# Splitting the first 128 tokens' convolution and drives into halves in a spiking decoder kernel, with one ScalarE job moved

## The reference

```
h    = rms(layernorm(x)) * w_norm
conv = conv_b + sum over j of 4: h[t - 3 + j] * conv_w[:, j]
h    = silu(conv)                               # 128 features
q, k, v = h @ wq, h @ wk, h @ wv                # 8 heads; q, k divided by their norms
sd   = h @ w_spike                              # the drives, 512 features
for t in 0 .. 511:                              # a recurrence over time
    mem  = 0.9 * mem + sd[t];  spike = mem > 0.5;  mem = mem - 0.5 * spike
    gates alpha[t], beta[t] from spike and from h;  the state is updated and read
```

## Time and profile before

| what | value |
|---|---|
| median of 3 runs | 1064.17 us (1058.85 to 1065.64) |
| profiled execution | 1070.31 us, span 1067.9 us |
| granted TensorE clock, mean | 0.966 |
| PE busy | 955.9 us, 90% |
| DVE busy | 693.0 us, 65% |
| ACT busy | 499.9 us, 47% |
| POOL busy | 181.4 us, 17% |

### The profile page before, as it was taken

One profiled execution on the slowest core, in us unless ns is written; L12 is line 12 of the kernel. 1 busy time (PEld: TensorE's weight loads), 2 busy tenths in 40 slices (PEclk: granted clock), 3 DMA queues, 4 the chain that ended last, 5 costly groups with the idle time before them and its releaser, 6 DMA issues. The chain is left out here.

```text
span 1067.9 us, 39931 instructions
## 1 busy us (share of the span) xinstructions
PE 955.9 (90%) x16658; PEld 641.8 (60%) x16658; DVE 693.0 (65%) x2418; ACT 499.9 (47%) x1506; POOL 181.4 (17%) x362
## 2 busy tenths in 40 slices
PE   7878769999999999999999887989999999999997
PEld 3333247777777777777777776656446446546542
DVE  2788787889899988988777665245435524724710
ACT  6667412555665555655556455433324324423311
POOL 7100100121121121221212211221210310310300
PEclk8999955999999999999999899989999999999999
DMA  3000000000000000000000104001000000000100
GB/s 99 1 1 1 1 2 3 4 4 4 4 5 4 5 4 4 5 4 4 4 4 5 30 5 129 3 10 28 7 1 23 22 0 18 27 1 4 31 0 10
DMA packets 18650, 13.81 MB, mean 13 GB/s; under 512 B 2491, under 2 KB 17259, under 8 KB 18475
## 3 DMA queue, kind: packets, MB, share of 16 engines
q1 hardware_dynamic: 18475, 11.28, 3.6%
HBM read 7.70 MB, written 1.05 MB: 8 GB/s over the span
## 5 line engine op out<-in xcount | busy, mean ns | idle before, releaser
L1105 PE MATMUL banks<-work 64*64 64x64 f32 x3072 | 100.2, 235 | 18.0 <-DVE gates L784 7.5
L1166 PE MATMUL banks<-work 64*64 64x32 f32 x2560 | 108.3, 224 | 8.9 <-ACT work L1568 5.0
L1166 PEld LDWEIGHTS banks<-work 64*64 64x64 f32 x2560 | 93.2, 139 | 21.7 <-issue 13.7
L203 DVE SCALAR_TENSOR_TENSOR mom<-gates 128x16 f32<-128x16 f32 x512 | 98.6, 193 | 11.2
L199 DVE SCALAR_TENSOR_TENSOR gates<-mom,gates 128x16 f32<-128x16 f32 x512 | 96.3, 188 | 11.9 <-ACT gates L1471 6.2
L784 DVE COPY_PREDICATED gates<-work,banks 128x256 f32<-128x256 uint32 x192 | 102.0, 531 | 1.1
L1498 ACT COPY work<-banks 128x128 f32<-128x128 f32 x160 | 43.6, 272 | 121.0 <-PE banks L1141 120.8
L1105 PEld LDWEIGHTS banks<-work 64*64 64x64 f32 x3072 | 74.8, 139 | 35.7 <-issue 26.0
L789 DVE TENSOR_TENSOR work<-work,banks 128x128 f32<-128x128 f32 x160 | 45.9, 287 | 74.9 <-PE banks L1166 71.5
L1141 PE MATMUL banks<-work,gates 64*64 64x32 f32 x2560 | 72.6, 218 | 6.2 <-issue 5.6
L661 POOL TENSOR_TENSOR mom<-mom 128x4 f32<-128x4 f32 x32 | 6.6, 207 | 418.1 <-ACT work L1547 418.1
(11 more groups left out here) (276 smaller groups left out, 2125.3 us busy)
## 6 DMA issues: line engine op xcount, KB each, us to landing
work<-gates SPq DMA_DIRECT2D x28, 38.5 KB
qT<-in_x_dram SPq DMA_DIRECT2D x4, 256.0 KB, 3.8
work<-in_x_dram SPq DMA_DIRECT2D x4, 256.0 KB, 2.9
out_dram<-work SPq DMA_DIRECT2D x4, 256.0 KB, 2.3
gates<-in_w_ff_dram SPq DMA_DIRECT2D x3, 256.0 KB, 3.6
wv_sb<-in_wv_dram SPq DMA_DIRECT2D x1, 512.0 KB, 4.7
work<-in_w_out_dram SPq DMA_DIRECT2D x1, 512.0 KB, 4.0
gates<-in_x_Wq_dram SPq DMA_DIRECT2D x1, 512.0 KB, 5.0
```

The lines of the kernel that those rows point to most:

```text
L203: ve.scalar_tensor_tensor(neg_mem, mem[:, :, t], 1.0, mem[:, :, t], ALU.is_gt, ALU.subtract)\
L1105: last = pe.matmul(level_out(l)[to, a], KS[rows, n.two, hp], late[rows, hp], start=True, stop=True)
L1166: last = pe.matmul(packed(psXT, l)[rows, a], Z[rows, l - 1, z], second_half(XT[:, n.two], l)[rows, a], start=True, stop=True)
```

## The change

Pair 0 is handled in two halves of 64 tokens (256 columns), and `stairs` moves on ACT from behind `centred(0)` to between `keep_qk(4, 2)` and `keep_h0(3)`. PE runs both half convolutions first, then the four drives of half 0, then those of half 1. The first charge needs only the four copies of half 0; the copies of half 1 are waited for at step 64. All later waits on `h_ok`, `sig_ok`, `conv_mm`, `sd_mm` and `sd_ok` are shifted by the added counts. Half 1 of a drive waits until the copy of half 0 of the same drive is out.

```
 charge(ve, t):
-            if t % PAIR == 0:
-                ve.wait_ge(sd_ok, HP * (t // PAIR + 1))
+            if t == 0:
+                ve.wait_ge(sd_ok, HP)
+            if t == PAIR // 2:
+                ve.wait_ge(sd_ok, drives_of(1))
+            if t and t % PAIR == 0:
+                ve.wait_ge(sd_ok, drives_of(t // PAIR + 1))
...
 vector:
-                keep_h(0)
+                keep_half_h(0)
+                keep_half_h(1)
...
 tensor:
+                def convolve_half(h):
+                    if h == 0:
+                        pe.wait_ge(h0_ok, 1)
+                        pe.wait_ge(consts, 6)
+                        pe.wait_ge(cw_ok, PAD + 1)
+                    for j in range(PAD + 1):
+                        at = h * (PAIR // 2) + j
+                        last = pe.matmul(half_bank(h, 0), conv_diag[:, j, :], h0T[:, :, at:at + PAIR // 2],
+                                         start=j == 0, stop=j == PAD)
+                    last.then_inc(conv_mm, 1)
...
+                def drive_half(n, h):
+                    pe.wait_ge(h_ok, h + 1)
+                    if h:
+                        pe.wait_ge(sd_ok, n + 1)
+                    pe.matmul(half_bank(drive_bank(n), h), wsp_sb[:, n, :], half_pair(hT[:, :], h), start=True, stop=True)\
+                        .then_inc(sd_mm, 1)
...
-                convolve(0)
-                for n in range(HP):
-                    drive_in(n)
+                convolve_half(0)
+                convolve_half(1)
+                for h in range(2):
+                    for n in range(HP):
+                        drive_half(n, h)
                 gate_in(0)
...
 scalar:
+                def soft_half(h):
+                    ac.wait_ge(conv_mm, h + 1)
+                    ac.activation(half_sig(h), half_bank(h, 0), ACT.Sigmoid, bias=v("conv_b")).then_inc(sig_ok, 1)
...
+                def keep_half_drive(n, h):
+                    ac.wait_ge(sd_mm, HP * h + n + 1)
+                    ac.mul(half_pair(aT[:, n], h), half_bank(drive_bank(n), h), 2.0).then_inc(sd_ok, 1)
...
                 centred(0)
-                stairs()
-                soft_conv(0)
-                for n in range(HP):
-                    keep_drive(n)
+                soft_half(0)
+                soft_half(1)
+                for h in range(2):
+                    for n in range(HP):
+                        keep_half_drive(n, h)
                 normal(1)
...
                 soft_conv(2)
                 keep_qk(4, 2)
+                stairs()
                 keep_h0(3)
```

More of the change, by code:

```diff
@@ L150, in zn, with half_sig @@
             return in_pair(kT[:, k], NPAIR - 2)
+        def half_sig(h):
+            return sig(0)[:, :, h * (PAIR // 2):(h + 1) * (PAIR // 2)]
         def sig(k):
@@ L181, in decoder_kernel @@
         NQ_ALL = NQK * NPAIR
-        NSD = HP * NPAIR
         AU_BANK, SS_BANK = 5, 4
@@ L193, in spread_bank, with pairs_of, drives_of, half_pair @@
             return ((0, 1, 6, 7) if k == 0 else (2, 3, 4, 7))[g]
+        def pairs_of(k):
+            return k + 1
+        def drives_of(pairs):
+            return HP * (pairs + 1)
+        def half_pair(t, h):
+            return in_pair(t, 0)[:, :, h * (PAIR // 2):(h + 1) * (PAIR // 2)]
+        def half_bank(i, at):
+            return by_batch(bank[i][:, at * (T // 2):(at + 1) * (T // 2)])
         def charge(ve, t):
             ve.wait_ge(fired, t + 1)
-            if t % PAIR == 0:
-                ve.wait_ge(sd_ok, HP * (t // PAIR + 1))
+            if t == 0:
[4 more added lines that the diff above has]
+                ve.wait_ge(sd_ok, drives_of(t // PAIR + 1))
             ve.scalar_tensor_tensor(mem[:, :, t], neg_mem, -0.9, mem[:, :, t], ALU.mult, ALU.add).then_inc(charged, 1)
@@ L631, in _ @@
                     gp.tensor_copy(EA[:, slot, 0], eye.unsqueeze(1).broadcast_to([P, HP, C])).then_inc(zeroed, 1)
-                gp.wait_ge(h_ok, NPAIR)
+                gp.wait_ge(h_ok, pairs_of(NPAIR))
                 gp.memset(Z, 0.0).then_inc(zeroed, 1)
@@ L689, in row_sums, with keep_half_h @@
                     ve.tensor_scalar(of_pair(neg_mean, k), of_pair(total, k), -1.0 / D, None, ALU.mult).then_inc(mean_ok, 1)
+                def keep_half_h(h):
+                    ve.wait_ge(sig_ok, h + 1)
+                    ve.scalar_tensor_tensor(half_pair(hT[:, :], h), half_bank(h, 0), v("conv_b"), half_sig(h), ALU.add, ALU.mult)\
+                        .then_inc(h_ok, 1)
                 def keep_h(k):
-                    ve.wait_ge(sig_ok, k + 1)
+                    ve.wait_ge(sig_ok, pairs_of(k + 1))
                     ve.scalar_tensor_tensor(in_pair(hT[:, :], k), by_batch(bank[k % 2]), v("conv_b"), sig(k), ALU.add, ALU.mult)\
@@ L1006, in turn_z @@
                     last.then_inc(zn_mm, 1)
+                def convolve_half(h):
[8 more added lines that the diff above has]
+                    last.then_inc(conv_mm, 1)
                 def convolve(k):
                     pe.wait_ge(h0_ok, k + 1)
[L1010 to L1014, removed]
+                    pe.wait_ge(h_ok, (2, pairs_of(k - 1))[k >= 2])
                     for j in range(PAD + 1):
@@ L1018, in convolve @@
                     last.then_inc(conv_mm, 1)
-                def drive_in(n):
[L1021 to L1026, removed]
+                def drive_half(n, h):
[4 more added lines that the diff above has]
+                        .then_inc(sd_mm, 1)
+                def drive_in(n):
+                    pe.wait_ge(h_ok, pairs_of(n // HP + 1))
+                    pe.wait_ge(qk_ok, NQK)
+                    pe.wait_ge(zT_ok, NPAIR)
+                    if n >= HP + 2:
+                        pe.wait_ge(sd_ok, HP + n - 1)
                     pe.matmul(bank[drive_bank(n)][:, :], wsp_sb[:, n % HP, :], in_pair(hT[:, :], n // HP), start=True, stop=True)\
@@ L1030, in gate_in @@
                 def gate_in(k):
-                    pe.wait_ge(h_ok, k + 1)
-                    pe.wait_ge(sd_ok, HP)
+                    pe.wait_ge(h_ok, pairs_of(k + 1))
+                    pe.wait_ge(sd_ok, drives_of(1))
                     if k:
@@ L1040, in project @@
                         if m < 2:
-                            pe.wait_ge(sd_ok, m + 1)
+                            pe.wait_ge(sd_ok, HP + m + 1)
                         else:
                             pe.wait_ge(sq_ok, m - 1)
-                        pe.wait_ge(h_ok, k + 1)
+                        pe.wait_ge(h_ok, pairs_of(k + 1))
                         pe.matmul(bank[project_bank(m)][:, :], (wq_sb if j < HP else wk_sb)[:, j % HP, :], in_pair(hT[:, :], k),
@@ L1065, in spread_norm @@
                         pe.wait_ge(h0_ok, NPAIR)
-                        pe.wait_ge(h_ok, NPAIR)
+                        pe.wait_ge(h_ok, pairs_of(NPAIR))
                     else:
@@ L1087, in level @@
                         pe.wait_ge(folded, NFOLD)
-                        pe.wait_ge(sd_ok, NSD)
+                        pe.wait_ge(sd_ok, drives_of(NPAIR))
                         pe.wait_ge(qk_ok, NQK)
@@ L1461, in keep_z @@
                     ac.copy(in_pair(zT[:, :], k), by_batch(bank[6 + k % 2])).then_inc(zT_ok, 1)
+                def soft_half(h):
+                    ac.wait_ge(conv_mm, h + 1)
+                    ac.activation(half_sig(h), half_bank(h, 0), ACT.Sigmoid, bias=v("conv_b")).then_inc(sig_ok, 1)
                 def soft_conv(k):
-                    ac.wait_ge(conv_mm, k + 1)
+                    ac.wait_ge(conv_mm, pairs_of(k + 1))
                     if k >= 2:
-                        ac.wait_ge(h_ok, k - 1)
+                        ac.wait_ge(h_ok, pairs_of(k - 1))
                     ac.activation(sig(k), by_batch(bank[k % 2]), ACT.Sigmoid, bias=v("conv_b")).then_inc(sig_ok, 1)
+                def keep_half_drive(n, h):
+                    ac.wait_ge(sd_mm, HP * h + n + 1)
+                    ac.mul(half_pair(aT[:, n], h), half_bank(drive_bank(n), h), 2.0).then_inc(sd_ok, 1)
                 def keep_drive(n):
-                    ac.wait_ge(sd_mm, n + 1)
+                    ac.wait_ge(sd_mm, HP + n + 1)
                     ac.mul(in_pair(aT[:, n % HP], n // HP), by_batch(bank[drive_bank(n)]), 2.0).then_inc(sd_ok, 1)
```

## The result

The changed kernel took 1070.75 us (median of 9 runs, 1061.23 to 1073.48), the kernel before 1063.45 us (9 runs, 1056.73 to 1066.72). Runs more than 1.5% slower than the fastest of their kernel are left out of all ratios; the largest took 1318.55 us at a granted clock of 0.644, in the second series with the gap filled.

The account below looks back on a forecast made before the run. PE, busy for 90% of the span, was taken to bound rounds and tail, whose start moves with ACT's list. -0.6 us plus 2.3 for the clock gave +1.7 on the median of 1064.17: 1065.9 us, range 1057.5 to 1071.5.

Parts of the forecast that it names:

- The sign, the bound and the mechanism: Slower by 1.7 us; PE bounds rounds and tail, their start follows ACT's list, and PE's longer idle gap lowers the clock.
- (c): Pair 0's drives run at the low clock in spite of the closed gap; 1069.2 us, chance 0.11.
- Part 1, the halves: Pair 0 in the prologue: no pause on PE, high clock kept, scan starts at 22.9, 5.7 us earlier.
- Part 2, ACT's list: ACT after the copies: `normal(1)` waits for POOL until 25.7, keeping 2.7 of 4.0 us; `convolve(2)` 3.9 us earlier, at 38.1.
- Part 3, the stairs: Stairs ahead of `keep_h0(3)` on ACT cost 3.35 us; 0.55 of 3.9 us is left, `convolve(3)` at 48.7; -0.6 us so far.
- Part 4, the clock: PE idles 4.8 us before `convolve(3)`, the clock falls, eight instructions take 6.01 us instead of 3.70: +2.3, bounds 0 to 3.7.
- Sum: -0.6 + 2.3 = +1.7: Shift of the whole kernel: -0.6 us up to the stairs, +2.3 for the clock's fall before `convolve(3)`.
- (a): The clock stays up through PE's gap before `convolve(3)`: -0.6 us, 1063.6 us, chance 0.22.
- (b): Low clock in the first rounds goes or gets shorter; all of it gone -7.4 us, 1056.8 us; chance 0.12.
- (d): Clock, once down at 46 to 49, stays down while ACT feeds PE in pieces; about +15.5, 1079.7 us; chance 0.05.

Follow-up runs that it names:

- the second series: Changed kernel, gap-filled version and others, compared again with the kernel before; the changed kernel took 1073.53 us, ratio 1.0048, the gap-filled version 1.0012.
- the last experiment: Six matmuls added in the second pass of the rounds, against the changed kernel with the stairs behind `keep_h0(3)`; 1056.92 us, 0.995 to the kernel before.

## Why the prediction was right, and where it was short

**The sign, the bound and the mechanism** were right. The median of 1070.75 lies in the range of 1057.5 to 1071.5, but 0.75 us from its upper end, and that it does is partly luck: the end was set by rival (c) and the scatter of the runs, and (c) did not happen.

**Part 1, the halves:** scan start 22.42 (forecast 22.9), last half copy out at 24.0 (24.5), PE without a pause, clock kept. Shown by the profile.

**Part 2, ACT's list:** `normal(1)` at 25.60, released by POOL (25.7 forecast); `convolve(2)` at 37.65 (38.1). Shown.

**Part 3, the stairs:** start at 44.17 (44.6), `convolve(3)` at 48.27 (48.7), DVE's wait at `keep_au(2)` 7.90 us where I had said above 4. The sum up to here was -1.0 at the convolution against the forecast -0.6. The halves alone and the stairs alone show both parts: `norm_root(1)` 3.6 us earlier and 6.3 later.

**Part 4, the clock:** idle time 4.76 us (4.8), fall in the gap in each of three profiles, convolution 5.1 to 6.3 us (6.0). Filling the gap removed it. The rule of the Trainium skill that I set against the row at 63.99 ("TensorE: Matmul & The Clock Gate", "Why this matters for your kernels") agrees with these traces for the gap of 4.76 us, which cost the clock in four profiles out of four. The falls behind pauses of about 2 us lie outside what it states. The row at 63.99 was the weaker witness, since the clock fell right behind the same idle time of 2.15 us in the changed kernel's first profile.

**The total was mis-sized.** The term "Sum: -0.6 + 2.3 = +1.7" measured +2.2 in the prologue on the average of three profiles, but +7.3 and +6.0 us in the medians. I took one fall in one gap as the whole of the clock's price. The changed kernel spends 14 us more at the low clock, 6.8 of it in the prologue: 3.4 to 6.8 in the gap (5.7 on average), 4.6 near 65 to 74 where the kernel before had 1.7, and 1.7 less in the drives. At 0.32 us for each us the surplus is worth 4.6 us, an estimate, of the 5.3 us in the means of the second series; so the term that was mis-sized is the low clock's (+2.3), and the sum fell short in it more than in anything else. That filling the gap brings back 5.4 us in the means shows that the gap is where the loss begins. It does not show a price beyond the prologue, since the interval (2.3 to 8.6) holds the 2.3 to 3.0 us by which `norm_root(1)` came earlier.

Two things stay open. Where the low clock behind 115 us adds up is not shown: three profiles are too few, and between the third round and the last, 468 to 477 us passed in profiles of one and the same changed kernel. And the halves may cost something in the rounds, a rival that I did not test: in all seven series of versions with the halves the mean lies above what the shift of `norm_root(1)` makes of it, by 0 to 6.3 us, 2.7 on average, while the two versions without them are at 0.1 and 0.7. Each of these numbers is uncertain by some 3 us.

**Rivals:** (a), the clock stays up through the gap, happened in no profile of the changed kernel. (b) was right in its price: two passes of the first rounds took 33.1 to 40.7 us, depending on the clock, and the last experiment collects 4.8 us of it. The changed kernel itself had 36.0 in its first profile and 40.6 and 40.5 in the others, so (b) came true in part in one execution. (c) and (d) did not happen.

## What to carry to other kernels

An instruction moved to another place in an engine's list is paid for where it stands in front of work that another engine waits for. Look for the place where its engine itself waits: here it was one instruction further on, and free. When PE's pause grows, count a fall of the clock as a cost of its own: here five matmuls thrown away in the pause made the kernel 5 to 6 us faster than leaving it empty. Compare as well how long all runs spend at the low clock, and not only the stretch that was changed. Where executions of a kernel differ by 1%, one profile shows the mechanism but not the size.

## What the runs showed of the hardware

- The granted clock fell within 4.76 us of idle PE in four profiles out of four. Around pauses of 1.6 to 2.2 us it fell in some executions and not in others at the same place: `drive_in` after 1.94 us ran mostly at the low clock (5.40 us for eight), after 1.63 us at the full one (3.70).
- In the first rounds PE was busy for 7.71 of 8 us from 150 to 158, mostly with 64 by 64 matmuls, and stayed at 1.2 GHz. With six matmuls of the full array ahead of them it was at 2.4 GHz from 146.8 to 160.5.
- Within one kernel, a run took 0.32 us longer for each us more at the low clock.
- Sixteen ACT instructions of 32 columns on PSUM took 1.55 us, 0.08 us apart when nothing waits between them.
